# Weighting gathered rows on VectorE, two tiles at once, in place of ScalarE, one tile at a time

## The chip, the cores and the metric

The kernel runs on one core of a Trainium2 chip. The metric is the device time of one execution in microseconds (us). Three executions of the kernel before took 5790.27, 5797.28 and 5843.74 us; the median is 5797.28 us.

## The reference, cut to what matters

Four graph layers follow each other on 3125 nodes of 256 features and 50000 edges that are sorted by their target. The first layer (L0) has three sublayers, and each sends every edge's source row, times the edge's weight, to the edge's target:

```
for l in range(3):
    h = x @ fc_w[l].T + fc_b[l]
    f = einsum('ncd,cde->nce', h.reshape(n, 4, 64) * norm_out, ch_w[l])
    m = f[src] * edge_w[:, None, None]          # 50000 rows of 256, each times one weight
    agg = segment_sum(m, dst, num_segments=n)
    x = relu(agg * norm_in + ch_b[l])
```

The layers behind it (L1, L3) take a maximum over edges with no weight, and L2 is an attention over the same edges. Everything is float32.

## The kernel before, in words

An edge pass walks the 50000 edges (50176 with padding) as 392 tiles of 128 partitions by 256 floats. Each partition holds its own chain of 392 consecutive edges. Four tiles make a group (`GT` = 4), so there are 98 groups (`NG`). The core does seven such passes. Three of them are weighted: e0, e1 and e2, one for each sublayer of L0. Pass e3 (L1) and e5 to e7 (L3) have no weights, and the attention pass (L2) is a function of its own. Node stages lie between the passes.

In a pass, GpSimd issues four indirect DMAs for each group (line 1356). They gather rows of the table in DRAM into the tiles of `G`. A weighted pass has six slots of four tiles (`sets` = 6). A slot comes free when `moved` says so: line 1350 waits until group g-6 has been moved, and the semaphore counts two for each group.

ScalarE moves (`move`, lines 1394 to 1405). It waits for the group's gathers, then for `linked` (the PSUM bank it is about to write, last read two groups before, must have been read), and runs four activations with a scale per partition. Each multiplies one 128x256 tile by its column of `WE` and writes half of a PSUM bank of `mv`; the second one of each pair counts `moved`. `mv` holds two groups.

VectorE links (`link`, lines 1416 to 1438): O[k] = O[k-1] * mask + mv[k], one scalar_tensor_tensor for each tile, each waiting for the one before. It waits for `moved` and, every second group, for the store of the ring slot that it overwrites. SyncE stores pairs of groups (line 1338) from the ring `O` of four groups to DRAM.

Each engine's order is written out. `pipelined` unrolls a list of (function, lead) pairs: at step s it calls each function for group s + lead, in the order of the list. All passes that stand here are flat, so every engine runs straight-line code of 98 steps. On ScalarE the list of a weighted pass is early, `(move, 0)`, late. On VectorE it is early, `(link, 0)`, late. Early and late are work "beside" the pass that has nothing to do with its rows.

In e1 and e2 that work is `rank_beside` (lines 860 to 944), a chain over three engines that does one block k in every two groups. VectorE makes one-hots (two instructions, line 270, late, at the odd step, three steps ahead). TensorE transposes them (`flip`, lines 913 and 914, eight matmuls), ScalarE copies them (`take`, lines 937 to 939, early, at the even step, ahead of its moves), TensorE multiplies them (`meet`, lines 923 to 925), and VectorE evaluates the result (`places`, lines 895 to 902, early, at the odd step, ahead of its links). TensorE's order is `meet` of block k at step 2k, `flip` of block k+1 at step 2k+1. `take` of block k waits for its `flip`; `meet` of block k waits for its `take` and for `places` of block k-1. `mlp_beside` adds four matmuls (line 1699) and one VectorE add (line 1706) in every third group, for 25 groups.

In e0 the work beside is `numbers_and_weights_beside`. Over the first 49 groups it has sixteen one-hot instructions for each group on VectorE (lines 755 and 756), then a number of short chains, and at groups 58 to 89 one scan for each group (line 794).

Of the kernel before, what the change touches and what calls it, by code (L numbers as in the profile page):

```python
# [8 lines left out]
ALU = mybir.AluOpType  # L9
ACT = mybir.ActivationFunctionType  # L10
AX = mybir.AxisListType
ds = bass.ds
# [8 lines left out]
GT = 4  # L21
# [130 lines left out]
def build(nc, a, out):  # L152
    top = ExitStack()
    Stage.used = []
    with top:
# [1128 lines left out]
        def edge_pass(name, index, ops, mask, weighted, beside=nothing_beside, picks=()):  # L1284
# [21 lines left out]
            with Stage(nc, name) as st:  # L1306
# [84 lines left out]

                @block.scalar
                def _(eng):
                    def move(g, q, turn):
                        if g < NG - 1:
                            got[g % sets].arrived(eng, dmas(g))
                        for h in range(2):
                            eng.wait_ge(linked, g * GT + (2 * h + 2))
                            bank = mv[:, 2 * (q % 2) + h, :]
                            for k in range(2):  # L1400
                                if g == NG - 1:
                                    tails[2 * h + k].arrived(eng, 1)
                                last = eng.activation(bank[:, k * D:(k + 1) * D], slot(g, 2 * h + k), ACT.Copy,  # L1403
                                                      scale=WE[:, ds(g * GT + (2 * h + k), 1)])
                            last.then_inc(moved, 1)

                    early, late = beside_on("scalar", eng)
                    steps = [*early, *([(move, 0)] if weighted else []), *late]
                    if steps:
                        pipelined(NG, U, eng, *steps, flat=flat)  # L1410

                @block.vector
                def _(eng):
                    eng.sem_inc(linked, 8)

                    def link(g, q, turn):
                        for k in range(GT):
# [19 lines left out]
                            behind = O[:, q % OB, k - 1, :] if k else O[:, (q - 1) % OB, GT - 1, :]  # L1437
                            eng.scalar_tensor_tensor(O[:, q % OB, k, :], behind, mask[:, ds(g * GT + k, 1)], here, op0, op1).then_inc(linked, 1)  # L1438

                    def lay_out(g, q, turn):  # L1440
                        if g in pick_of:
                            i = pick_of[g]
                            if i >= 2:
                                eng.wait_ge(spread, i - 1)
                            eng.tensor_scalar(diag[:, i % 2, :], ident[:, :], node_of[:, g:g + 1], None, ALU.mult).then_inc(laid, 1)
# [15 lines left out]
                        eng.wait_ge(keyed, 2)  # L1461
                    picking = [(lay_out, 7), (one_hots, 5)] if picks else []
                    early, late = beside_on("vector", eng)
                    pipelined(NG, U, eng, *early, *picking, (link, 0), *late, flat=flat, head=0 if flat else U)
                    if "vector_end" in side:
                        side["vector_end"](eng)
            for q in range(sets):
# [807 lines left out]
```

## Time and profile before

| what | value |
| --- | --- |
| three executions | 5790.27, 5797.28, 5843.74 us |
| the profiled execution's own time | 5809.64 us |
| its span (first to last instruction) | 5807.9 us |
| PE, DVE, ACT, POOL busy | 2840.8, 3248.1, 1029.9, 3239.7 us |
| gathers of e0: first and last start | 110.9 and 717.1 us |
| gathers of e1 | 814.1 and 1444.1 us |
| gathers of e2 | 1542.7 and 2173.2 us |
| gathers of e3 | 2336.4 and 2921.3 us |

In the profile PE is TensorE, DVE is VectorE, ACT is ScalarE, POOL is GpSimd, SP is SyncE. Times are us from the start of the span. "Idle before" is the time that an engine stood still ahead of an instruction, and the arrow names what ended it; "issue" stands where no wait that the profile shows ended it, "remote" where the release came from something that the profile doesn't know. A matmul's start is recorded, its end is modelled.

### The profile page before, as it was taken

How to read it: one execution, taken by the hardware profiler on the slowest of the kernel's cores; microseconds unless marked ns; L12 is line 12 of the kernel's file. 1: busy time of each engine (PE TensorE's matmuls, PEld its weight loads, DVE VectorE, ACT ScalarE, POOL GpSimd, SP SyncE). 2: the span in 40 equal slices, each digit the busy share in tenths (PEclk: the TensorE clock that was granted, in tenths of full speed). 3: DMA queues.
4: the chain of work that ended last, by engine and by line, in shares of the span. 5: the costliest groups of instructions: out<-in, count | busy, mean ns of one | idle time of the engine just before them, and what ended most of it. 6: DMA issues, size and time to landing. Idle time of an engine off the chain costs nothing. (4 is left out here: it accounts for less than half of the span.)

```text
span 5807.9 us, 44153 instructions
## 1 busy us (share of the span) xinstructions
PE 2840.8 (49%) x11716; PEld 2035.6 (35%) x11716; DVE 3248.1 (56%) x9230; ACT 1029.9 (18%) x2648; POOL 3239.7 (56%) x3351
## 2 busy tenths in 40 slices
PE   5111045544455446454451000477676777578675
PEld 4110033333333334221131000356455655466554
DVE  5577434444344445477875777635454555445554
ACT  4223323333233333000011111210001000010002
POOL 5556645555455553666736666246562666536662
PEclk8555565555655557675665555688787988788776
DMA  3445545544455441355524665235452555435552
GB/s 115 156 158 176 183 130 174 168 165 162 132 171 167 169 160 59 126 173 174 184 95 148 192 196 191 75 123 182 167 179 100 170 189 187 157 101 192 186 178 96
DMA packets 284843, 900.76 MB, mean 155 GB/s; under 512 B 70731, under 2 KB 123320, under 8 KB 241464
## 3 DMA queue, kind: packets, MB, share of 16 engines
q0 software_dynamic: 157728, 428.39, 25.5%
q1 hardware_dynamic: 126872, 469.63, 21.0%
q8 instruction: 93, 1.52, 0.1%
q14 instruction: 150, 1.23, 0.1%
HBM read 445.41 MB, written 452.35 MB: 155 GB/s over the span
## 5 line engine op out<-in xcount | busy, mean ns | idle before, releaser
L1356 POOL DMA_INDIRECT WORK<-table,SRCI x1376 | 1315.9, 956 | 1023.2 <-issue 476.2
L1356 POOL DMA_INDIRECT WORK<-table,BYSRC x1092 | 1064.9, 975 | 831.1 <-issue 551.2
L1382 PE MATMUL e_pm<-ARENA 128*128 128x256 f32 (+1 forms) x4200 | 1110.0, 416 | 291.4 <-issue 287.6
L1382 PEld LDWEIGHTS e_pm<-ARENA 128*128 128x128 f32 (+1 forms) x4200 | 860.4, 209 | 518.2 <-issue 402.3
L1438 DVE SCALAR_TENSOR_TENSOR WORK<-WORK,NST,e_mv 128x256 f32<-128x256 f32 x1173 | 562.4, 479 | 411.7 <-issue 199.9
L1438 DVE SCALAR_TENSOR_TENSOR WORK<-WORK,LOWE 128x256 f32<-128x256 f32 x1288 | 626.1, 486 | 103.1 <-remote 38.6
L1403 ACT ACTIVATE e_mv<-WORK,WE 128x256 f32<-128x256 f32 x1176 | 485.9, 458 | 316.7 <-DVE WORK L1438 247.0
L1824 POOL DMA_INDIRECT WORK<-table_attention,SRCI x392 | 375.0, 957 | 181.4 <-issue 127.9
L1438 DVE SCALAR_TENSOR_TENSOR WORK<-WORK,LOWE,e_pm 128x256 f32<-128x256 f32 x84 | 40.3, 480 | 680.3 <-remote 341.5
L923 PE MATMUL e_rb<-ARENA 98*128 98x128 bf16 x392 | 114.8, 293 | 621.0 <-ACT ARENA L939 508.9
L1455 DVE TENSOR_TENSOR ARENA<-e_pr,ARENA 128x640 f32<-128x640 f32 x420 | 314.2, 812 | 69.0 <-remote 41.9
L987 PE MATMUL e_hi<-ARENA 128*128 128x392 bf16 x392 | 180.8, 461 | 332.8 <-DVE ARENA L973 185.1
L923 PEld LDWEIGHTS e_rb<-ARENA 98*128 98x128 bf16 x392 | 95.6, 244 | 648.3 <-ACT ARENA L939 598.5
L895 DVE SCALAR_TENSOR_TENSOR ARENA<-e_rb,upto 128x128 bf16<-128x128 f32 x392 | 90.6, 287 | 380.6 <-remote 338.7
L2013 PE MATMUL comb<-ident,WORK 128*8 128x128 f32 x1 | 0.4, 372 | 595.1 <-PEq L149 595.1
L925 PE MATMUL e_ra<-ARENA 98*128 98x32 f32 x784 | 249.0, 412 | 0.0
L1356 POOL DMA_INDIRECT ARENA<-table,SRCI x192 | 192.1, 1001 | 89.2 <-issue 56.4
L1544 ACT ACTIVATE WORK<-bn_ps 128x256 f32<-128x256 f32 x3 | 1.2, 384 | 1236.3 <-PE bn_ps L1027 1236.3
L925 PEld LDWEIGHTS e_ra<-ARENA 98*128 98x128 f32 x784 | 196.2, 310 | 45.9
L2013 PEld LDWEIGHTS comb<-ident,WORK 128*8 128x8 f32 x1 | 0.1, 84 | 595.2 <-issue 595.2
L1169 PE MATMUL n_x<-WORK 128*128 128x256 f32 x200 | 79.8, 492 | 261.8 <-DVE WORK L1088 195.5
L937 ACT ACTIVATE ARENA<-e_rt 98x512 bf16<-98x512 bf16 x98 | 58.5, 597 | 824.3 <-remote 649.7
(383 smaller groups left out, 5413.0 us busy)
## 6 DMA issues: line engine op xcount, KB each, us to landing
edge_results<-WORK SPq DMA_DIRECT2D x336, 1024.0 KB
edge_results_attention<-WORK SPq DMA_DIRECT2D x98, 544.0 KB
WORK<-table,SRCI POOLq DMA_INDIRECT x1376
table<-ARENA SPq DMA_DIRECT2D x28, 640.0 KB, 3.3
WORK<-table,BYSRC POOLq DMA_INDIRECT x1092
turned_layers<-WORK SPq DMA_DIRECT2D x50, 128.0 KB, 1.7
HTT<-turned_layers SPq DMA_DIRECT2D x50, 128.0 KB
WORK<-table_attention,SRCI POOLq DMA_INDIRECT x392
```

Source lines behind the costliest of these rows:

```text
L895: eng.scalar_tensor_tensor(rank_tmp[:, n, :], pb[:, n * P:(n + 1) * P], 2.0, upto[:, :], ALU.is_equal, ALU.mult, accum_out=rank[:, 0, n:n ...
L923: eng.matmul(pb[:, cols], rank_t[0:HI, b, 0, cols], rank_t[0:HI, b, 0, cols], start=True, stop=False)
L925: last = eng.matmul(pa[:, n * LO:(n + 1) * LO], rank_tf[0:HI, b, cols], HIST[0:HI, ds((k + first) * RB + n, 1), :].rearrange("p o l -> p ( ...
L937: eng.activation(rank_t[0:HI, b, 0, :], turned_hot[0:HI, 0, :], ACT.Copy)
L987: last = eng.matmul(sums[d][:, :], oh_pay[:, q % 2, n, d, :], oh_place[:, q % 2, n, :], start=False, stop=False)
L1169: eng.matmul(xps[:, t % 2, 0:D], SEL[:, slot, :], CARRY if crossing else ENDS, start=True, stop=True).then_inc(crossed, 1)
L1356: eng.indirect_dma_start(slot(g, k), None, T, bass.IndirectOffsetOnAxis(ap=index[:, t:t + 1], axis=0)).then_inc(landed, 16)
L1382: last = eng.matmul(made_ps[:, i % 4, 0:D], hot_rows[0:n, i % 2, j, :], AGG[0:n, j, :], start=j == 0, stop=j == NT - 1)
L1403: last = eng.activation(bank[:, k * D:(k + 1) * D], slot(g, 2 * h + k), ACT.Copy, scale=WE[:, ds(g * GT + (2 * h + k), 1)])
L1438: eng.scalar_tensor_tensor(O[:, q % OB, k, :], behind, mask[:, ds(g * GT + k, 1)], here, op0, op1).then_inc(linked, 1)
L1455: eng.tensor_tensor(hot_rows[:, i % 2, at, :], rows_ps[:, i % 2, 0:P].unsqueeze(1).broadcast_to([P, CH, P]), key[:, at].unsqueeze(2).broad ...
L1824: eng.indirect_dma_start(G[:, q * GT + k, :], None, T2, bass.IndirectOffsetOnAxis(ap=SRCI[:, t:t + 1], axis=0)).then_inc(got[q].sem, 16)
```

## The change

ScalarE's `move` is removed. VectorE gets `scale` with a lead of one group: at step s it scales group s+1 and then links group s. One instruction multiplies two gathered tiles (128x512) by their two columns of `WE`, each column stretched over 256 elements by the access pattern, and writes a whole PSUM bank. `scale` stands behind the early steps and ahead of `link`. It waits for `linked` up to all links of group g-2, and for the gathers; each of its two instructions counts `moved`, so the totals that GpSimd and `link` wait for stay as they were. The buffers, the six slots and the ring stay as well.

```diff
@@ block.scalar
-                    def move(g, q, turn):
-                        if g < NG - 1:
-                            got[g % sets].arrived(eng, dmas(g))
-                        for h in range(2):
-                            eng.wait_ge(linked, g * GT + (2 * h + 2))
-                            bank = mv[:, 2 * (q % 2) + h, :]
-                            for k in range(2):
-                                if g == NG - 1:
-                                    tails[2 * h + k].arrived(eng, 1)
-                                last = eng.activation(bank[:, k * D:(k + 1) * D], slot(g, 2 * h + k), ACT.Copy,
-                                                      scale=WE[:, ds(g * GT + (2 * h + k), 1)])
-                            last.then_inc(moved, 1)
-
                     early, late = beside_on("scalar", eng)
-                    steps = [*early, *([(move, 0)] if weighted else []), *late]
+                    steps = [*early, *late]
@@ block.vector
+                    def scale(g, q, turn):
+
+                        if g >= 2:
+                            eng.wait_ge(linked, g * GT + (8 - GT))
+                        if g < NG - 1:
+                            got[g % sets].arrived(eng, dmas(g))
+                        for h in range(2):
+                            if g == NG - 1:
+                                for k in range(2):
+                                    tails[2 * h + k].arrived(eng, 1)
+                            at = g % sets * GT + 2 * h
+                            eng.tensor_tensor(mv[:, 2 * (q % 2) + h, :].rearrange("p (k d) -> p k d", k=2), G[:, at:at + 2, 0:D],
+                                              WE[:, ds(g * GT + 2 * h, 2)].unsqueeze(2).broadcast_to([P, 2, D]), ALU.mult).then_inc(moved, 1)
+
@@
-                    pipelined(NG, U, eng, *early, *picking, (link, 0), *late, flat=flat, head=0 if flat else U)
+                    pipelined(NG, U, eng, *early, *([(scale, 1)] if weighted else []), *picking, (link, 0), *late, flat=flat, head=0 if flat else U)
```

## Rows read from the trace of the kernel before

**Rows 1.** The page, parts 1 and 5: engines, and the line that goes.
```profile
PE 2840.8 (49%) x11716; PEld 2035.6 (35%) x11716; DVE 3248.1 (56%) x9230; ACT 1029.9 (18%) x2648; POOL 3239.7 (56%) x3351
...
L1403 ACT ACTIVATE e_mv<-WORK,WE 128x256 f32<-128x256 f32 x1176 | 485.9, 458 | 316.7 <-DVE WORK L1438 247.0
```
**Rows 2.** Stretches e0, e1, e2, e3, attention: PE, PEld, DVE, ACT, POOL busy, PEclk, DMA.
```profile
110.00:735.00 625.00, 69.42 (x510) 53.79 (x510) 383.54 (x1412) 173.73 (x405) 374.21 (x392) 0.50 0.51 170
812.00:1466.00 654.00, 321.01 (x1277) 204.26 (x1277) 303.27 (x1056) 230.22 (x539) 371.28 (x392) 0.50 0.49 163
1540.00:2196.00 656.00, 321.96 (x1278) 205.06 (x1279) 303.89 (x1059) 230.21 (x539) 372.20 (x393) 0.50 0.48 163
2330.00:2960.00 630.00, 279.90 (x924) 124.89 (x921) 446.05 (x1541) 10.59 (x29) 391.06 (x392) 0.64 0.49 161
3090.00:3650.00 560.00, 0.00 (x0) 0.00 (x0) 418.84 (x1004) 66.64 (x336) 371.50 (x389) 0.50 0.59 187
```
**Rows 3.** Line 1356 (gathers) in e1: durations, then its engine's idle time by releaser.
```profile
L1356 POOL DMA_INDIRECT WORK<-table,SRCI x392: 941/947/1052, 814.1 to 1444.1; - x196
...
  ACT e_mv L1403: 147.4, 24
```
**Rows 4.** The same of line 1356 in e0.
```profile
L1356 POOL DMA_INDIRECT WORK<-table,SRCI x392: 940/947/2631, 110.9 to 717.1; - x196
...
  ACT e_mv L1403: 112.8, 29
```
**Rows 5.** The same of line 1356 in e3, a pass without weights.
```profile
  DVE WORK L1438: 80.6, 16
```
**Rows 6.** Timeline of POOL in e1: first and last of 16 gathers, and the next.
```profile
1122.05 0.94 POOL L1356 DMA_INDIRECT WORK<-table,SRCI  x1 [6.51 <-ACT e_mv L1403]
...
1140.81 0.94 POOL L1356 DMA_INDIRECT WORK<-table,SRCI  x1 [0.30 <-issue]
1148.18 0.94 POOL L1356 DMA_INDIRECT WORK<-table,SRCI  x1 [6.42 <-ACT e_mv L1403]
```
**Rows 7.** Timeline of ACT over the same cycle.
```profile
1127.33 3.25 ACT L1403 ACTIVATE e_mv<-WORK,WE 128x256 f32<-128x256 f32 x8
1144.81 0.60 ACT L937 ACTIVATE ARENA<-e_rt 98x512 bf16<-98x512 bf16 x1 [14.23 <-remote]
```
**Rows 8.** Timeline of DVE over the same cycle.
```profile
1130.33 0.42 DVE L1706 TENSOR_TENSOR X<-e_mlp,X 128x256 f32<-128x256 f32 x1
1139.09 0.29 DVE L895 SCALAR_TENSOR_TENSOR ARENA<-e_rb,upto 128x128 bf16<-128x128 f32 x1 [8.34 <-remote]
...
1140.67 2.10 DVE L1438 SCALAR_TENSOR_TENSOR WORK<-WORK,NST,e_mv 128x256 f32<-128x256 f32 x4
1142.68 0.76 DVE L270 TENSOR_TENSOR ARENA<-ARENA,iota_b 128x392 bf16<-128x392 bf16 x2
```
**Rows 9.** Timeline of PE over the same cycle: the last matmuls of meet and flip.
```profile
1130.77 0.64 PE L925 MATMUL e_ra<-ARENA 98*128 98x32 f32 x2
...
1132.95 0.29 PE L914 MATMUL e_rt<-identb,ARENA 128*32 128x128 bf16 x1
```
**Rows 10.** Timeline of DVE early in e0: two instructions with no wait.
```profile
142.29 0.28 DVE L755 TENSOR_SCALAR ARENA<-iota_b,BYSRC 128x98 bf16<-128x98 bf16 x1 [1.17 <-issue]
143.69 0.23 DVE L756 TENSOR_SCALAR ARENA<-iota_b,ARENA 128x32 bf16<-128x32 bf16 x1 [1.12 <-issue]
```
**Rows 11.** Timeline late in e0: two groups, by their scans.
```profile
599.25 1.03 DVE L794 TENSOR_TENSOR_SCAN ARENA<-e_hd,start_src,ARENA 98x392 f32<-98x392 f32 x1
...
606.25 1.03 DVE L794 TENSOR_TENSOR_SCAN ARENA<-e_hd,start_src,ARENA 98x392 f32<-98x392 f32 x1
```
**Rows 12.** DVE's groups by form in e0.
```profile
L755 DVE TENSOR_SCALAR ARENA<-iota_b,BYSRC 128x98 bf16<-128x98 bf16 x392 | 101.2, 267 | 23.3 <-issue 23.1
```
**Rows 13.** Timeline of DVE in the attention pass: two products of the same form.
```profile
3308.05 1.26 DVE L1936 TENSOR_TENSOR att_g<-WORK,att_p 128x512 f32<-128x512 f32 x2
```
**Rows 14.** POOL's gathers in the attention pass: busy, mean ns, idle by releaser.
```profile
L1824 POOL DMA_INDIRECT WORK<-table_attention,SRCI x389 | 372.2, 957 | 180.5 <-issue 127.0 <-DVEq L1940 53.5
```

## The prediction

> **What bounds the kernel now.** I read the page first, then the busy times by stretch, then who waits for whom at the gathers, then one cycle on every engine. On the page no engine is busy above 56% and the line that goes, 1176 activations, is 485.9 us of ScalarE, an engine busy 18% of the span [rows 1]. So the change can only pay through a wait. By stretch, each weighted pass takes 625 to 656 us for 392 gathers, e3 takes 630 and the attention pass about 560, and in none of them is VectorE or GpSimd full [rows 2].
>
> Line 1356 says why. In e1 GpSimd waits 24 times for ScalarE, 147.4 us, and is otherwise busy or issuing: 482.6 us without those waits, 1.23 us for a gather [rows 3]. The 24 waits are alike. A cycle is 26.13 us (1122.05 to 1148.18): 16 gathers, four groups, in 19.7 us to the end of the last, and a pause of 6.42 us [rows 6]. In the pause ScalarE isn't working: its last move ends at 1130.6, and it stands 14.23 us until `take` starts at 1144.81 [rows 7]. `take` waits for `flip`, whose last matmul is recorded at 1132.95 [rows 9]. VectorE in the same way starts `places` at 1139.09 after 8.34 us, though `meet` is recorded as done at 1131.4 [rows 8, 9]. Both idles are "remote". So TensorE's results come 8 to 12 us later than the trace models them, and everything in order behind `take` or `places` waits with it.
>
> The same slowness shows in the open on VectorE in e0. Two one-hots with no wait start 1.40 us apart, where one takes 0.27 us [rows 10, 12]; late in e0 a group of ten VectorE instructions takes exactly 7.0 us, 0.70 each, while gathers run on [rows 11]. I read one pattern: while GpSimd issues gathers, an engine gets through some 70 to 80 instructions at full speed, then only one per 0.70 us, and full speed returns about 3 us after GpSimd pauses (last gather over at 1141.75, `take` at 1144.81) [rows 6, 7]. The count is an estimate: attention has about 72 VectorE instructions for each of its pauses (1004 in 14 cycles of 24 to 32 gathers) and e1, with 44 a cycle, never slows on VectorE [rows 2, 14]. In e1 the engine that runs dry is TensorE, with 53 matmuls and 53 loads a cycle.
>
> **The change part by part.**
>
> *Removed:* 392 activations a pass from ScalarE. In e1 and e2 `take` already starts the moment it is released, so rank work gains nothing. What goes is the tie of the slots to `flip` and `take`.
>
> *Added:* two VectorE instructions a group. Attention has two of this form in 1.26 us, PSUM output included [rows 13]; I take 1.26 us a group, 123 us a pass. They free the slots, so they lie on GpSimd's path. Does VectorE become the bound? In e1 two groups cost it `places` 1.58 us (1139.09 to 1140.67), links 4.2, one-hots 0.76, the add 0.28 (0.42 in two of three) [rows 8], and now 2.52: 9.3 us, against 10.0 us for eight gathers at 1.25. It fits, barely. Its instructions rise from 44 to about 52 a cycle: below the 70.
>
> *Moved:* a slot is now freed behind `places` of the block before, so behind `meet`, no longer behind `flip` and `take`. `meet` comes one TensorE step earlier, which sounds like a gain, but the cycle is tied to GpSimd's own pause. Walk it: GpSimd's last gather ends; TensorE is released 3.06 us later [rows 6, 7]; what is left of a slow `meet` finishes; `places` 1.58; the two products 1.26; GpSimd resumes. Before, the same path was 3.06 plus 3.37 for `take` and four moves. How much of `meet` is left is the unknown. Block k+1 comes about 7 us after the release, at full speed (flip 1.8, `take` 1.5, `meet` 3.7, from rows 7 and 9 and the spacing of matmuls there); then TensorE is dry and the next flip and meet are 24 matmuls at 0.70, about 19 us with `take`. That is 26 us from the release, and the next release comes at 3.06 + 2.84 + 19.7 = 25.6 us. So some 0.4 us is left: pause 6.3, cycle 26.1. Bounds: nothing left and a pause as in the passes that VectorE already frees, 80.6/16 = 5.0 us in e3 [rows 5], gives -1.2 us a cycle, -30 a pass; a whole `meet` left, 3.7 us, gives a pause of 9.6, +3.2 a cycle, +76 a pass. I take 0.
>
> *Behind the waits:* `scale` waits for its gathers ahead of the links, the one-hots and, through order, the next `places`. Where GpSimd leads by four groups, as here, they have landed. SyncE's stores wait for links, which come 1.3 us a group later; the ring has two groups of room, so this costs nothing unless VectorE falls under GpSimd's pace. At the end of a pass the backlog of about five groups is worked off by VectorE alone: 5 x 1.26 = +6 us in each pass.
>
> *GpSimd itself:* its gather takes longer beside VectorE instructions that read SBUF twice. In e1 a gather costs 1.23 us without waits; in e3, where all four links and the one-hots do so or run fast modes, (584.9 - 80.6)/391 = 1.29 [rows 3, 5] (584.9: last start of e3 minus the first, from the table). Attention's product reads only one SBUF tensor, so no row has the new form: 0 to 0.056 us a gather, 0 to 22 us a pass. Two instructions in place of sixteen: I take 7 us a pass.
>
> The Trainium skill ("SBUF — State Buffer", on the shared port pair) says that a VectorE instruction with two SBUF inputs and a GpSimd instruction that reads SBUF lock each other out fully. By it each product could hold a gather off for its whole length; that is the rival C below, and e3's 1.29 speaks for a small share of it.
>
> *e0:* early, VectorE has 16 one-hots and four links, about 4.4 us a group at full speed, 5.7 with the products, above GpSimd's 5.0. But time goes in cycles as in e1: about 80 fast instructions, then slow until GpSimd pauses. With 26 instructions a group in place of 23 a cycle holds 3.3 groups, not 4; the slots run out sooner and the pause is shorter (GpSimd's waits there are 112.8/29 = 3.9 us [rows 4]). I make it -10 us over 49 groups. Late, a slow group goes from ten instructions to thirteen, 7.0 to 9.1 us [rows 11]: GpSimd's lead of four groups is used up after nine gathered groups in place of fourteen, a pause restores the speed, and 25 groups come out near 6.4 us in place of 5.5. +24 us. With the 6 and 7 us from above, e0 is +27. Bounds: -50 (the pace of attention) and +123 (all products on the path).
>
> *Sum:* e0 +27, e1 and e2 each 0 + 6 + 7 = +13, in all +53 us on the profiled execution's 5809.6, 5863. That execution is 12.4 us above the median of the runs, so the forecast is about **5850 us**, +0.9%. All else in the kernel (e3, attention, e5 to e7, node stages) is untouched.
>
> **The rivals.** A measurement of this kernel can tell about 1% from no change, 58 us.
>
> *A, faster.* The pauses belong to ScalarE's order (`take` ahead of the moves), and a pass freed by VectorE runs like attention: 53.5 us of waits in 389 gathers against 147.4 [rows 3, 14]. For: attention has the same products on VectorE and a stretch of 560 us. Against: it has no TensorE work at all [rows 2]. Each of e1 and e2 would gain 60 to 90 us, e0 up to 30: about 5640.
>
> *B, slower.* `meet` becomes the tie that decides the pause. If more than about 1 us of it is left at the release, the pause passes 7 us; VectorE at 9.3 of 10 us has no room to catch up. A whole `meet`, +76 a pass, and e0 at +60 give about 6020. For: the 8.34 us wait for it [rows 8] is in VectorE's order now, ahead of the slots. Against: it comes a step ahead of `flip`.
>
> *C, GpSimd locked out.* 588 products, up to 0.63 us each: +370, about 6170. Against: e3's 0.056 us a gather.
>
> *D.* The change doesn't move the bound at all: 5800.
>
> **How the numbers follow.** My forecast with D as its flat variant, between 5780 and 5900, has 0.54; A 0.22; B 0.21; C 0.03. Faster by over 1%: 0.22 from A. Slower by over 1%: B and C 0.24 and a fifth of the forecast, 0.10: 0.34. Within 1%: 0.44. The range leaves half of A's far end and half of B's and all of C out: 5690 to 5990. The forecast's own range is 5780 to 5900.
>
> **What would show it.** ScalarE has 147 activations in e1 and VectorE 196 products of about 0.68 us. Right: GpSimd's waits in e1, now for VectorE, are 22 to 26, of 5.5 to 7 us, in cycles of 16 gathers; VectorE's idle is ahead of line 895; e1's gathers take 625 to 645 us. The walk of the cycle is wrong if the pauses come every 24 gathers (A) or last 9 us (B), or if a gather between pauses costs over 1.29 us (C). e0 shows the late part: scans 9.1 us apart where they are slow. If e0's gathers end sooner than 606 us after they start, the step that counts instructions is wrong.

## The result, and the profile after

The changed kernel takes 5751.59 us, the median of 4 runs (5731.99 to 5771.79), against 5804.25 for the kernel before: a ratio of 0.9895, 95% interval 0.9862 to 0.9928. I had forecast 5850 us, slower by 0.9%. By the ratio it is faster by 1.05%; the two medians lie 0.9% apart. The profiled execution takes 5771.79 us, 37.9 less than the one before.

Page of the kernel after, part 1, and the new group of part 5:

```profile
PE 2826.7 (49%) x11716; PEld 2024.7 (35%) x11716; DVE 3584.6 (62%) x9818; ACT 554.0 (10%) x1472; POOL 3315.3 (57%) x3351
...
L1438 DVE TENSOR_TENSOR e_mv<-WORK,WE 128x512 f32<-128x512 f32 x588 | 383.2, 697 | 52.6 <-DMA WORK<-table,SRCI 45.1
```

ScalarE lost 1176 activations and 476 us, VectorE gained 588 products and 336 us [rows 1]. GpSimd, whose instructions are the same, is busy 75.6 us more. That is a price of the change, and it stands on an engine whose instructions the diff doesn't touch.

GpSimd's group of line 1356 in e1 (busy us, mean ns, idle before by releaser), first of the kernel before, then of the kernel after with the count of its waits for VectorE:

```profile
L1356 POOL DMA_INDIRECT WORK<-table,SRCI x392 | 371.3, 947 | 306.3 <-ACT e_mv L1403 147.4 <-issue 112.3 <-POOLq L149 46.6
```
```profile
L1356 POOL DMA_INDIRECT WORK<-table,SRCI x392 | 394.0, 1005 | 255.8 <-issue 117.1 <-DVE e_mv L1438 91.4 <-POOLq L149 46.2
...
  DVE e_mv L1438: 91.4, 15
```

So e1 is a sum of two: the waits fall from 147.4 to 91.4 us (-56.0), the gathers' own time rises from 371.3 to 394.0 (+22.7), and "issue" by 4.8; one wait of 1.1 us is new and labelled remote. That makes -27.4; the gathers of e1, first start to last, take 602.5 us (793.8 to 1396.3) in place of 630.0. e2 is the same (604.1 for 630.5), and in e0 the waits fall from 112.8 to 59.9 and the gathers grow from 374.2 to 402.1:

```profile
L1356 POOL DMA_INDIRECT WORK<-table,SRCI x392 | 402.1, 1026 | 215.6 <-issue 155.6 <-DVE e_mv L1438 59.9
```

which gives 578.3 us for 606.3. The cycle of e1 is no longer the one of [rows 6]. GpSimd's timeline after, the first gather behind each of three pauses in a row:

```profile
1117.92 0.94 POOL L1356 DMA_INDIRECT WORK<-table,SRCI  x1 [5.71 <-DVE e_mv L1438]
...
1154.97 0.94 POOL L1356 DMA_INDIRECT WORK<-table,SRCI  x1 [5.75 <-DVE e_mv L1438]
...
1191.95 0.94 POOL L1356 DMA_INDIRECT WORK<-table,SRCI  x1 [5.72 <-DVE e_mv L1438]
```

A cycle is 37.0 us and holds 24 gathers; before it was 26.1 us and 16. The pause is 0.7 us shorter, and there are 15 in place of 24. VectorE's and ScalarE's side of one of these pauses, behind a last gather that ends at 1149.2:

```profile
1151.82 0.29 DVE L895 SCALAR_TENSOR_TENSOR ARENA<-e_rb,upto 128x128 bf16<-128x128 f32 x1 [8.57 <-remote]
...
1153.39 1.30 DVE L1438 TENSOR_TENSOR e_mv<-WORK,WE 128x512 f32<-128x512 f32 x2
```
```profile
1151.91 0.60 ACT L937 ACTIVATE ARENA<-e_rt 98x512 bf16<-98x512 bf16 x1 [14.40 <-remote]
```

The end of a pause is as in [rows 7, 8]: everybody stands, and 2.6 us after GpSimd's last gather both engines start within 0.1 us of each other. Now `places` and one group's products are all that is left to do (1151.82 to 1154.7), and GpSimd goes on.

**Where the 37.9 us between the two profiles are.** e0 -28.0, e1 -27.5, e2 -26.4, together -81.9. The stretches behind them grow: from the last gather of e0 to the first of e1 97.0 becomes 104.7, behind e1 98.6 becomes 103.7, behind e2 163.2 becomes 165.5: +15.1. Most of it is the end of the pass: from the end of the last gather to the end of the last link it takes 14.7, 18.1 and 18.2 us before and 23.2, 22.3 and 22.3 after. The rest, +29, is in passes whose code is the same: e3 +3.4, attention +2.8, e5 -9.7, e6 +19.1, e7 +12.0. Those are the pauses' own scatter: in a second pair of profiles (runs 5 and 6) e5 to e7 went the other way, 1662.7 us before and 1650.4 after. So the change is worth 67 us in the first pair of profiles (81.9 less 15.1) and 68 in the second (89.6 less 21.1, counted the same way), and the rest is scatter.

### The profile page after: what moved, and what is told of

Read it like the earlier page. It is cut to its first block and busy times, and to the rows that moved or that the text cites. A ratio compares the mean times of both kernels' runs of the same rounds, so it can differ in the third digit from the quotient of the medians.

```text
span 5770.0 us, 43557 instructions
## 1 busy us (share of the span) xinstructions
PE 2826.7 (49%) x11716; PEld 2024.7 (35%) x11716; DVE 3584.6 (62%) x9818; ACT 554.0 (10%) x1472; POOL 3315.3 (57%) x3351
## 5 line engine op out<-in xcount | busy, mean ns | idle before, releaser
L1356 POOL DMA_INDIRECT WORK<-table,SRCI x1376 | 1390.7, 1011 | 864.0 <-issue 481.4
L1438 DVE TENSOR_TENSOR e_mv<-WORK,WE 128x512 f32<-128x512 f32 x588 | 383.2, 697 | 52.6 <-DMA WORK<-table,SRCI 45.1
L925 PEld LDWEIGHTS e_ra<-ARENA 98*128 98x128 f32 x784 | 196.2, 310 | 45.8
L1954 DVE SCALAR_TENSOR_TENSOR WORK<-WORK,NST,att_g 128x256 f32<-128x256 f32 x343 | 164.9, 481 | 57.4 <-remote 12.6
L987 PEld LDWEIGHTS e_hi<-ARENA 128*128 128x128 bf16 x392 | 48.3, 123 | 432.8 <-DVE ARENA L973 240.0
```

The lines of the kernel that those rows point to most:

```text
L925: last = eng.matmul(pa[:, n * LO:(n + 1) * LO], rank_tf[0:HI, b, cols], HIST[0:HI, ds((k + first) * RB + n, 1), :].rearrange("p o l -> p ( ...
L987: last = eng.matmul(sums[d][:, :], oh_pay[:, q % 2, n, d, :], oh_place[:, q % 2, n, :], start=False, stop=False)
L1356: eng.indirect_dma_start(slot(g, k), None, T, bass.IndirectOffsetOnAxis(ap=index[:, t:t + 1], axis=0)).then_inc(landed, 16)
L1438: eng.tensor_tensor(mv[:, 2 * (q % 2) + h, :].rearrange("p (k d) -> p k d", k=2), G[:, at:at + 2, 0:D], WE[:, ds(g * GT + 2 * h, 2)].unsqu ...
L1954: eng.scalar_tensor_tensor(OA[:, i, t, 0:D], OA[:, i, t - 1, 0:D] if t else scaled_row, NST[:, ds(b * BT + t, 1)], here, ALU.mult, ALU.add ...
```

## The experiments

One thing has to be said first. The runs fell on seven chips, and they are of two kinds. On four of them the kernel before takes 5789 to 5826 us, with the pauses described above. On three it takes 4708 or 4709 us and **has no pause at all**. The lines below say which it was. What differs in these chips or in how they are set up, no trace shows. The packets of the gathers' queue take alike on both: 25.5% of sixteen engines' 5807.9 us in the kernel before and 31.2% of their 4717.9 us in run 7, 1481 and 1472 us. Runs 1 and 7 differ from the kernel before only in ScalarE's order, so run 7 stands in for its profile on such a chip. It is 1090 us shorter: 796 of them in the eight passes of gathers, the other 294 between and around the passes, where GpSimd issues such DMAs as well (line 1068).

| run | chip | kernel us | before us | ratio, 95% interval | e1 gathers us | mean gather ns |
|---|---|---|---|---|---|---|
| 1, 7 moves ahead | no pauses | 4712.67; 4718.13 | 4707.74; 4709.11 | 1.0012 [1.0002, 1.0022]; 1.0020 [1.0009, 1.0031] | 491.2; 490.4 | 952; 950 |
| 11 moves ahead | pauses | 5840.52 | 5800.41 | 1.0086 [1.0056, 1.0116] | 641.7 | 962 |
| 2, 8 idle moves | no pauses | 4812.02; 4810.12 | same as 1; 7 | 1.0217 [1.0200, 1.0234]; 1.0214 [1.0197, 1.0231] | 515.5; 514.8 | 1013; 1012 |
| 12 idle moves | pauses | 5697.01 | 5800.41 | 0.9836 [0.9793, 0.9878] | 593.9 | 1006 |
| 3, 10 scale by tile | no pauses | 4763.99; 4769.82 | same as 1; 7 | 1.0115 [1.0098, 1.0131]; 1.0124 [1.0107, 1.0141] | 491.7; 490.9 | 953; 951 |
| 4, 9, 17 eight slots | no pauses | 4805.18; 4810.93; 4802.12 | 4707.74; 4709.11; 4708.93 | 1.0206; 1.0209; 1.0203 [1.0186, 1.0220] | 512.6; 513.1; 511.6 | 1006; 1007; 1004 |
| 5 after again | pauses | 5745.67 | 5816.95 | 0.9895 [0.9850, 0.9939] | 596.7 | 1006 |
| 6 before again | pauses | 5837.93 (one) | 5816.95 | - | 631.5 | 947 |
| 13 flip twice | pauses | 5736.12 | 5788.82 | 0.9909 [0.9887, 0.9932] | 597.3 | 1009 |
| 14 split | pauses | 5779.02 | 5788.82 | 0.9977 [0.9960, 0.9994] | 602.5 | 949 |
| 15 paced | pauses | 5830.94 | 5826.24 | 1.0008 [0.9981, 1.0035] | 625.9 | 946 |
| 16 rests | pauses | 5729.04 | 5826.24 | 0.9854 [0.9793, 0.9916] | 598.7 | 958 |
| 18 rests, more | no pauses | 5164.37 | 4708.93 | 1.0974 [1.0955, 1.0992] | 597.5 | 955 |

**Runs 1, 7 and 11: ScalarE's moves ahead of `take`.** Kernel before, one line:

```diff
-                    steps = [*early, *([(move, 0)] if weighted else []), *late]
+                    steps = [*([(move, 1)] if weighted else []), *early, *late]
```

> The kernel before, with one change of order: ScalarE still scales the rows with its 392 activations a pass, but one group ahead, and its moves stand ahead of take in its queue, so that a slot is freed behind places of the block before, as in the changed kernel. Theory ORDER (what the change brought is that the slots no longer hang behind flip and take): GpSimd's pauses in e1 come every 24 gathers instead of 16, 15 to 17 of them of 5.5 to 6 us in place of 24 of 6.1, and the gather stays at 1.235 us, so e1's gathers take 575 to 595 us in place of 630; the kernel 5620 to 5700 us, faster than both. Theory COUNT (an engine, or all of them together, gets through a fixed number of instructions between pauses, and the change took 392 activations off that number): nothing changes, pauses every 16 gathers, e1 625 to 635 us, the kernel 5780 to 5830.

> The kernel of run 1 once more (the moves on ScalarE one group ahead, ahead of take), on a chip where the kernel before has its pauses and takes about 5800 us, if the call gets one. Theory ORDER: pauses every 24 gathers in e1 and e2, 15 to 17 of them, gathers at 1.235 to 1.256 us, e1 575 to 595 us, ratio 0.97 to 0.985. Theory COUNT (ScalarE's activations shorten the cycle): pauses every 16, e1 620 to 635 us, ratio 0.99 to 1.005. Without pauses on this chip: as in run 1, ratio 1.001.

> The kernel of runs 1 and 7 (the moves stay on ScalarE, one group ahead and ahead of take); both of those fell where the kernel before has no pauses. With pauses: theory ORDER expects them every 24 gathers in e1 and e2, 15 to 17 of them, gathers at 1.235 to 1.256 us, e1 575 to 595 us, ratio 0.97 to 0.985; theory COUNT expects every 16 gathers, e1 620 to 635 us, ratio 0.99 to 1.005. Without pauses: ratio 1.001 to 1.002.

Runs 1 and 7 fell on chips without pauses and say only that the order costs 0.1 to 0.2% there. GpSimd's group in e1 of run 7:

```profile
L1356 POOL DMA_INDIRECT WORK<-table,SRCI x392 | 372.3, 950 | 140.7 <-issue 114.8 <-POOLq L149 21.6 <-ACT e_mv L1403 4.3
```

No wait for ScalarE is left in 392 gathers but 4.3 us, and the pass takes 490 us, where the pass of [rows 3], on a chip with pauses, took 630. Run 11 is the test. Its group in e1:

```profile
L1356 POOL DMA_INDIRECT WORK<-table,SRCI x392 | 377.2, 962 | 312.2 <-ACT e_mv L1403 152.1 <-issue 113.4 <-POOLq L149 46.8
...
  ACT e_mv L1403: 152.1, 22
```

22 waits of 6.9 us, still one in 16 gathers. Theory ORDER falls: the tie to `take` and `flip` was not what held the cycle at 16, and with it falls the explanation that I would have given for the gain.

**Runs 2, 8 and 12: activations put back on ScalarE on which nothing depends.** Kernel after, e1 and e2:

```diff
-                    steps = [*early, *late]
+                    spare, = carve(AGW_BASE[:, 4600:6648], ((2, GT, D), F32))
+
+                    def idle_moves(g, q, turn):
+                        for h in range(2):
+                            if g >= 2:
+                                eng.wait_ge(idled, 2 * (g - 2) + h + 1)
+                            for k in range(2):
+                                last = eng.activation(spare[:, q % 2, 2 * h + k, :], MB[:, :], ACT.Copy)
+                            last.then_inc(idled, 1)
+                    steps = [*early, *([(idle_moves, 0)] if name in ("e1", "e2") else []), *late]
```

> The changed kernel, with as many activations put back on ScalarE in e1 and e2 as before the change, at the same place behind take and with as many waits and signals, but on constant rows into spare memory, so that no slot depends on them. Theory ORDER: no effect, e1's gathers 600 to 605 us with pauses every 24 gathers, the kernel 5730 to 5770. Theory COUNT with ScalarE's instructions in the common number: pauses every 16 to 20 gathers again, e1 over 615 us, the kernel 5780 to 5850. Theory COUNT by engine (only TensorE's own number matters): as ORDER.

> The kernel of run 2 once more (the changed kernel with 392 activations put back in e1 and e2 on which nothing depends). With pauses: ORDER expects every 24 gathers, e1 595 to 605 us, as the changed kernel; COUNT expects cycles of 16 to 20 gathers and over 615 us. Without pauses: ratio 1.022 as in run 2.

> The kernel of runs 2 and 8 (the changed kernel, with 392 activations put back in e1 and e2 on which nothing depends). With pauses: ORDER expects them every 24 gathers, e1 595 to 605 us, ratio 0.985 to 0.995, as the changed kernel; COUNT expects cycles of 16 to 20 gathers and over 615 us, ratio 0.995 to 1.01. Without pauses: ratio 1.021.

Run 12, e1:

```profile
L1356 POOL DMA_INDIRECT WORK<-table,SRCI x392 | 394.4, 1006 | 247.3 <-issue 114.6 <-DVE e_mv L1447 85.9 <-POOLq L149 46.7
```

16 waits, 85.9 us: with ScalarE as loaded as before the change, the cycle stays at 24 gathers. Freeing ScalarE is not what the change gave. In e2 of this run the 16 waits are shorter, 72.7 us in all, and the pass takes 581.6 us where the changed kernel's takes 604; why is open. Runs 2 and 8 show the changed kernel's code, whole, with these activations added, on chips without pauses: slower than before by 2.1%.

**Runs 3 and 10: one large SBUF input per product.** Kernel after:

```diff
-                            at = g % sets * GT + 2 * h
-                            eng.tensor_tensor(mv[:, 2 * (q % 2) + h, :].rearrange("p (k d) -> p k d", k=2), G[:, at:at + 2, 0:D],
-                                              WE[:, ds(g * GT + 2 * h, 2)].unsqueeze(2).broadcast_to([P, 2, D]), ALU.mult).then_inc(moved, 1)
+                            for k in range(2):
+                                last = eng.tensor_scalar(mv[:, 2 * (q % 2) + h, k * D:(k + 1) * D], slot(g, 2 * h + k),
+                                                         WE[:, ds(g * GT + 2 * h + k, 1)], None, ALU.mult)
+                            last.then_inc(moved, 1)
```

> The changed kernel, but each product is made for one tile, by a tensor_scalar with the weight as a column per partition: four instructions of 128x256 a group with one large SBUF input in place of two of 128x512 with two SBUF inputs. Theory CONTENTION (a gather is stretched while VectorE reads two SBUF inputs): the mean gather in e1 falls from 1.005 to 0.95-0.96 us and the cost without pauses from 1.300 to 1.235-1.25; with pauses unchanged that is 18 to 25 us less in each weighted pass, the kernel 5670 to 5710. Rival (any VectorE work on slots or into PSUM stretches them, or the links do): the gather stays at 0.99 to 1.01 us, the kernel 5740 to 5790. Two more instructions a group could shorten the cycle if VectorE's count decides: pauses every 20 gathers.

> The kernel of run 3 once more (four products a group, each with one large SBUF input). Run 3 had gathers of 0.953 us in e1 against 1.006 to 1.013 in runs 2 and 4. With pauses: the gather back at 0.95 and 1.24 to 1.26 without pauses, so e1 is 15 to 25 us shorter than the changed kernel's 597 to 603 if the pauses stay every 24 gathers, ratio 0.975 to 0.985 with e0 no worse; if eight more VectorE instructions a cycle shorten it to 20 gathers, 595 to 615 us. Without pauses: ratio 1.011 as in run 3.

GpSimd in e1, of run 10 and then of run 17, which has the two-input products of the change; both without pauses, so that a pass is nothing but its gathers (the last two slots of run 17 lie in another tensor, so its gathers stand in two groups):

```profile
L1356 POOL DMA_INDIRECT WORK<-table,SRCI x392 | 372.7, 951 | 140.7 <-issue 117.6 <-POOLq L149 21.6 <-DVE e_mv L1438 1.5
```
```profile
L1356 POOL DMA_INDIRECT WORK<-table,SRCI x296 | 297.5, 1005 | 112.0 <-issue 89.9 <-POOLq L149 22.1
L1356 POOL DMA_INDIRECT ARENA<-table,SRCI x96 | 95.9, 999 | 29.2 <-issue 29.2
```

951 ns against 1004, and 1013 and 1012 in runs 2 and 8, whose slots are six. Contention is shown: the same multiplication, at the same place on the same engine, with one large input costs GpSimd nothing in e1 (490.9 us, as run 7), and with two it costs 21 us. The products of run 10 are also shorter (128x256), so length would be a rival; the attention pass rules it out, below. In e0 the four smaller instructions cost as much as contention did (549.5 us in run 10, 548.4 in run 17): there VectorE is full, and run 10 waits 15 times, 45.8 us.

The trace shows how it happens. After, GpSimd and VectorE in e1:

```profile
1124.56 0.94 POOL L1356 DMA_INDIRECT WORK<-table,SRCI  x1 [0.30 <-issue]
1125.81 1.33 POOL L1356 DMA_INDIRECT WORK<-table,SRCI  x1 [0.30 <-issue]
1127.44 0.94 POOL L1356 DMA_INDIRECT WORK<-table,SRCI  x1 [0.30 <-issue]
```
```profile
1125.03 1.30 DVE L1438 TENSOR_TENSOR e_mv<-WORK,WE 128x512 f32<-128x512 f32 x2
```

The products end at 1126.33, and the gather that started inside them at 1125.81 ends at 1127.14, 0.81 us later. The gather before it was under way when the products began, and took its 0.94. Over e1, 78 of the 392 gathers start inside a product and last 1.245 us on average; the other 314 last 0.946, as before the change. Each of the 78 ends 0.81 to 0.87 us after the product in which it began. The products last 0.69 us on average whether a gather is under way at their start or not. So a gather is held only if it begins during a product, until about the product's end, and then still needs 0.81 us.

The attention pass of the kernel before has products of the same form and length, but with one input in PSUM. A gather of it that begins inside such a pair, and the pair:

```profile
3304.02 0.95 POOL L1824 DMA_INDIRECT WORK<-table_attention,SRCI  x1 [0.30 <-issue]
...
3303.89 1.28 DVE L1936 TENSOR_TENSOR att_g<-WORK,att_p 128x512 f32<-128x512 f32 x2
```

79 gathers of that pass begin inside a product, and they last 0.946 us. So it is the second SBUF input that holds a gather, not the product's length.

The Trainium skill ("SBUF — State Buffer", section "SBUF: two separate sides") says that a VectorE instruction with two SBUF inputs and a GpSimd one that reads SBUF exclude each other: whichever starts first has the shared pair of ports for its whole instruction. For the gathers that begin inside a product, the trace agrees. That a gather under way holds the product back, it does not show (0.69 us either way), and there the measurement decides.

**Runs 4, 9 and 17: eight groups of slots in e1 and e2** (two more, behind the rank work's part of the arena; kernel after):

```diff
-            sets = SETS if weighted or picks else DEEP
+            sets = 8 if name in ("e1", "e2") else SETS if weighted or picks else DEEP
```

> The changed kernel with 8 groups of slots in place of 6 in e1 and e2. Theory SLOTS (GpSimd runs through its slots while everything behind TensorE stands, so the cycle is as long as the slots allow): pauses every 32 gathers, about 12 of 5.7 us in place of 16, e1 575 to 585 us, the kernel 5700 to 5725. Theory COUNT (a number of instructions between pauses): pauses stay every 24 gathers, or TensorE's results come late for longer and the pause stays, e1 598 to 606 us, the kernel 5735 to 5770.

> The kernel of run 4 once more (8 groups of slots in e1 and e2). With pauses: theory SLOTS expects cycles of 32 gathers, 11 to 13 pauses of 5 to 6 us, e1 575 to 590 us; COUNT expects cycles of 24 gathers or a pause no shorter in the sum, 595 to 605 us. Without pauses: ratio 1.020 as in run 4.

> The kernel of runs 4 and 9 (the changed kernel with 8 groups of slots in e1 and e2), for a chip with pauses. Theory SLOTS (after VectorE stops getting results on time, GpSimd runs on until its slots are used up, so two more groups make the cycle 32 gathers): 11 to 13 pauses of 5 to 6.2 us, e1 391 x 1.30 + 70 = 575 to 590 us, ratio 0.975 to 0.985. Rival ONSET (what decides is when the others' lateness begins, and it ends only with a pause): cycles stay at 24 gathers or become uneven, e1 597 to 610 us, ratio 0.985 to 0.995.

All three fell on chips without pauses, so the question that they were for stays open. What they give is what the change costs where nothing pauses: e0 takes 548.4 us in run 17 and 492.3 in run 18, whose e0 is the code before; e1 511.6 against 490.4 to 491.2. That is +56, +21 and +21, 98 us in all, and the kernel is 2.0% slower (93 us). The changed kernel by itself was not run on such a chip.

**Runs 5 and 6: both kernels again.**

> The changed kernel itself, timed again. In the four runs above no pass of GpSimd's gathers had the pauses of 5 to 6 us that the first profiles show, and the kernel before took 4708 us, so the same chip type can run this kernel with and without them. Theory PAUSES (the gain came from fewer pauses, its price is longer gathers): where the pauses are absent, only the price is left: gathers of 1.005 us in e1 and e2 and about 1.07 in e0, 20 to 23 us longer in e1 and in e2, 55 us longer in e0, the kernel 1.018 to 1.024 of before; where the pauses are there, 0.985 to 0.995 of before, as first measured. Rival (the gain doesn't come from pauses at all): under 1.000 in both conditions.

> The kernel before itself, for its profile beside the changed kernel's on one chip. Without pauses: e0, e1 and e2 at 1.256 us a gather, 491 to 493 us a pass, no wait for ScalarE of over 1.5 us, 4700 to 4715 us. With pauses: as first profiled, 606, 630 and 630 us, 5790 to 5850 us.

With pauses, 0.9895 once more, with e0, e1 and e2 at 579.2, 596.7 and 604.4 us after and 608.3, 631.5 and 630.1 before. That is what theory PAUSES expects where there are pauses. Its other side, 1.018 to 1.024 without them, is seen only in kernels that add something to the changed one (runs 2, 4, 8, 9 and 17: 1.020 to 1.022).

**Run 13: each flip's transposes twice.** Kernel after:

```diff
-                        for n in range(RB):
+                        for n in (*range(RB), *range(RB)):
                             eng.transpose(turned_hot[0:HI, 0, n * P:(n + 1) * P], rank_hi[:, b, n, :], identb[:, :])
```

> The changed kernel, with the eight transposes of each flip issued twice in e1 and e2 (392 more matmuls with their loads in a pass; the second set writes the same values). TensorE isn't full: 1277 matmuls in a pass of about 600 us. Theory TENSORE (after a pause TensorE works at full speed for a limited number of matmuls, then at 0.70 us each until the next pause): 1277 matmuls fit as 725 at the slow pace in 508 us of gathers and 16 x 34.5 after pauses; 1669 then need about 27 pauses, every 14 to 16 gathers, and e1 takes 650 to 680 us, ratio 1.00 to 1.02. Theory LINKS (VectorE's or the slots' own state sets the cycle, TensorE's count does not matter): pauses stay every 24 gathers, e1 597 to 610 us, ratio 0.985 to 0.995. On a chip without pauses: no effect, ratio 1.02 to 1.023.

```profile
L1356 POOL DMA_INDIRECT WORK<-table,SRCI x392 | 395.6, 1009 | 249.3 <-issue 114.5 <-DVE e_mv L1438 88.3 <-POOLq L149 46.5
```

392 more matmuls with their loads in the pass don't shorten the cycle: 16 waits, 88.3 us, 24 gathers a cycle. That takes away the core of my reading of the trace, that in e1 TensorE "runs dry" after some 53 matmuls.

**Run 14: the change in e1 and e2 alone, by tile** (the products of runs 3 and 10; in e0 ScalarE scales).

> The change in e1 and e2 alone, and there with four products a group of one tile each (one large SBUF input); in e0 ScalarE scales as before. Without pauses: e0 492 us, e1 and e2 491 us, so the price of the change is gone, ratio 0.999 to 1.002. With pauses: e0 as before (606 us), gathers in e1 and e2 at 0.95 us and 1.25 us without pauses. If the cycle stays at 24 gathers, e1 and e2 580 to 590 us and ratio 0.983 to 0.988; if four more VectorE instructions a block of two groups shorten it to 20 gathers, 595 to 610 us and 0.99 to 0.995.

```profile
L1356 POOL DMA_INDIRECT WORK<-table,SRCI x392 | 372.1, 949 | 277.8 <-issue 112.4 <-DVE e_mv L1450 109.5 <-POOLq L149 46.4
```

The gathers are back at 949 ns, and with them the cycle is back at 16 gathers (22 pauses of 5.4 us): what contention no longer costs is paid in pauses, and e1 takes 602.5 us, as with the change. Behind its gathers more is left to do: from the last gather of e1 to the first of e2 it takes 115.5 us (98.6 before, 103.7 after), behind e2 175.5 (163.2 and 165.5). So the kernel is only 0.2% faster than before, where 0.5 to 1.7% were expected. Two things differ from the change here, the second input and the number of products in a group, four in place of two. This run doesn't separate them.

**Run 15: a memset behind each gather.** Kernel before, e1 and e2: `eng.memset(AGW_BASE[:, 4600 + t:4601 + t], 0.0)`.

> The kernel before, with one small memset (128x1) on GpSimd behind each gather of e1 and e2, so that a gather costs 1.30 to 1.37 us instead of 1.235; ScalarE still moves the rows. Theory PACE (a slower gather lets the other engines run on time longer, and that made 16 gathers into 24): pauses every 24 gathers, 15 or 16 of them of 6 us, e1 391 x 1.30 to 1.37 + 95 = 600 to 630 us, ratio 0.99 to 1.00. Rival FORM (the number or the engine of the scaling instructions decides, the pace doesn't): pauses stay every 16 gathers, e1 391 x 1.30 to 1.37 + 147 = 655 to 685 us, ratio 1.01 to 1.02. On a chip without pauses: 508 to 536 us, ratio 1.007 to 1.02.

The experiment failed in its aim. The memset (0.12 us) fell into the 0.30 us of issue, and a gather still cost 1.235 us. The cycles became shorter (29 pauses of 4.9 us in place of 24 of 6.1), the sum of the pauses stayed, 143 us, and so did the pass, 626 us.

**Run 16: GpSimd breaks off by itself.** Kernel before, e1 and e2:

```diff
+                        if name in ("e1", "e2") and g % 3 == 2:
+                            for h in range(2):
+                                if g > 2 or h:
+                                    eng.wait_ge(rested, 2 * (g // 3) + h)
+                                eng.memset(AGW_BASE[:, 4600:6500], 0.0).then_inc(rested, 1)
```

> The kernel before, with GpSimd breaking off by itself after every 12 gathers in e1 and e2, for two memsets of 128x1900 in a row (3.4 us by the 1.37 us of 128x1536 at the kernel's start), before the slots are used up. Theory RELEASE (the other engines come back to speed 3 us after GpSimd stops its gathers, whatever it does meanwhile): hardly a wait for ScalarE is left, e1 391 x 1.235 + 32 x 3.5 = 595 us in place of 630, ratio 0.985 to 0.99. Rival (GpSimd must be idle, or the others' lateness comes from something else): the rests add up, e1 630 + 50 to 110 us, ratio 1.02 to 1.04. On a chip without pauses: 491 + 110 us, ratio 1.045.

GpSimd's timeline and its group in e1:

```profile
1123.34 0.95 POOL L1356 DMA_INDIRECT WORK<-table,SRCI  x1 [0.30 <-issue]
1124.29 3.43 POOL L1362 MEMSET ARENA<- 128x1900 f32 x2
1127.88 0.95 POOL L1356 DMA_INDIRECT WORK<-table,SRCI  x1 [0.15 <-issue]
...
L1356 POOL DMA_INDIRECT WORK<-table,SRCI x392 | 375.4, 958 | 160.4 <-issue 113.1 <-POOLq L149 46.1 <-ACT e_mv L1408 1.2
```

147.4 us of waits have become 1.2, for 108 us of memsets; e1 takes 598.7 us where 595 was expected. It looks as if on such a chip the gathers need stops of some 3 us, and GpSimd pays less if it stops early than if it is stopped: a forced pause is 6.1 us because behind the release stand `take` and four moves. GpSimd need not be idle in the stop; memsets do. The lateness isn't gone altogether: VectorE still has 16 remote waits of over 1 us in e1, but they add up to 36.8 us and none is longer than 2.6, where before they were 27 with 184.1 us. Part of the gain lies behind the gathers: from the last of e1 to the first of e2 it takes 88.0 us in place of 98.6. This kernel, the one before with rests added to GpSimd's program, is as fast as the changed one (0.9854 and 0.9895, intervals that overlap).

**Run 18: rests in e3 and e5 to e7 as well**, six memsets of 128x512 behind every 20 gathers.

> The kernel of run 16 (GpSimd breaks off for 3.4 us after every 12 gathers in e1 and e2; ScalarE scales as before), and in e3 and e5 to e7 it breaks off as well, for six memsets of 128x512 (about 3.2 us) after every 20 gathers. Theory RELEASE: no wait of over 1.5 us for VectorE is left there, e3 391 x 1.29 + 19 x 3.4 = 569 us in place of 585, e5 to e7 363 x 1.27 + 18 x 3.4 = 522 in place of 543 to 566; ratio 0.965 to 0.98. Rival (20 gathers are already past the point where the others are late, so the rest ends in the same backlog): waits of 1 to 3 us stay behind the rests, e5 to e7 540 to 560 us, ratio 0.98 to 0.99.

It met a chip without pauses, where a rest is pure cost: 1.097. But its e1 takes 597.5 us there, and run 16's takes 598.7 on a chip with pauses. With the rests in, e1 takes the same on both kinds of chip. Whether they help in e3 and e5 to e7 where there are pauses, this run can't say.

## Why the prediction was wrong, step by step

- **"The cycle is tied to GpSimd's own pause" and stays at 26.1 us: wrong, and most of the error.** The walk through the end of the pause was right: a release about 3 us behind the last gather (2.6), `places` 1.57, two products 1.3, in all 5.7 us with 0.3 of issue, where I had 6.3. But its other half, when the next lateness begins, rested on a count of instructions, and I held that count fixed. It isn't fixed: the cycle grew to 24 gathers, 37.0 us, and the pauses fell from 24 to 15. Had it stayed at 16, e1 would by this estimate have had 24 pauses of 5.7 us and come out at 630 + 23 - 11, about 642.
- **The count itself.** "70 to 80 instructions, then one per 0.70 us" describes VectorE in e0 [rows 10 to 12], but as a rule it is refuted for TensorE (run 13) and for ScalarE (run 12). Its support was also misread. Attention before has 16 pauses of over 1.5 us, in cycles of 16 to 28 gathers, not 14 of 24 to 32, so 63 VectorE instructions for each and not 72. And the units differ: of the "ten VectorE instructions" between two scans in [rows 11] the trace counts five (four links and a scan), while the 44 and 72 are such counted instructions. Nor is VectorE's own number fixed: the trace has 43 of them in the cycle of [rows 6] and 77 in one after. The sign set for this step, e0's gathers over in under 606 us, came true: 578.3.
- **Contention, "I take 7 us a pass" within 0 to 22: mis-sized.** It is 22.7 us in e1 with pauses, three times the term and just above its upper bound, 21 without, and 28 (56 without pauses, with what VectorE's fullness adds) in e0. I divided by instructions ("two in place of sixteen"); what counts is the share of time in which a gather can begin inside a product: 196 products, 0.60 us apart within a pair, cover about 118 of 602 us, a fifth, and 78 of 392 gathers is a fifth.
- **The backlog, +6 a pass: right in size.** From the last gather to the last link it takes 8.5, 4.2 and 4.1 us more in e0, e1 and e2. Its reason, five groups times 1.26 us, isn't shown: that time is 34.2 us in e1 of run 14 and 4.6 in run 16, so it depends on how late the other engines are when the pass ends, and without pauses e1 has 8.5 us (run 17) against 12.3 (run 7).
- **e0, +27 us: wrong in sign (-28.0).** Its first 49 groups gained 20.8 us, where I had put 10; the late part then gained 7.2, where I had put a loss of 24. The price of a slow group was nearly right, 9.1 forecast and 9.8 measured between the scans, but only three groups pay it, where before 17 or so stand 7.0 apart [rows 11]. Timeline of VectorE late in e0, first where I expected slow groups, then where they are:

```profile
590.41 1.03 DVE L794 TENSOR_TENSOR_SCAN ARENA<-e_hd,start_src,ARENA 98x392 f32<-98x392 f32 x1
594.55 1.03 DVE L794 TENSOR_TENSOR_SCAN ARENA<-e_hd,start_src,ARENA 98x392 f32<-98x392 f32 x1
...
662.32 1.03 DVE L794 TENSOR_TENSOR_SCAN ARENA<-e_hd,start_src,ARENA 98x392 f32<-98x392 f32 x1
672.12 1.03 DVE L794 TENSOR_TENSOR_SCAN ARENA<-e_hd,start_src,ARENA 98x392 f32<-98x392 f32 x1
```

  The nine pauses behind the first scan, 24.0 us, have become one of 2.4. It is the same step that failed: lateness begins later than a fixed count says.
- **Rival A** named the sign that I had set, pauses every 24 gathers. But its reason, ScalarE's order, fell in run 11, and its size, 60 to 90 us in each of e1 and e2, left out contention: the waits fell by 56 us in e1, the pass by 27.
- **Rival C** is right as a mechanism and wrong in its size: a product holds a gather, but only one that begins inside it. The sign set for it, a gather of over 1.29 us between pauses, came true as well: 1.30.

**What stays open** is why the lateness begins later in the changed kernel. Shown: it is neither the tie to `take` (run 11), nor ScalarE's load (12), nor TensorE's count (13), and it does go with the two-input form, or with two products a group in place of four (14). What goes along in all of these is the gathers' own cost: cycles of 16 gathers where a gather costs 1.235 to 1.252 us without waits (before, runs 11 and 14), of 24 where it costs 1.30 (after, runs 5, 12 and 13) and about 23 in e3 before, at 1.29. It would fit that gathers which follow each other more slowly let the others run on time for longer, and then the contention pays for itself. But run 15, meant to slow the gathers alone, did not slow them, so this is argued, not shown, and other passes speak against it as the whole reason: attention before has mostly cycles of 24 gathers at 1.26 us, e5 to e7 mostly of 26 at 1.27. What makes the other engines late at all is open too. That they wait for the loading of their own instructions was not tested: the instruction queues carry the same 28 packets during e1's gathers in the kernel before and in run 7, at 0.1% of the DMA engines' time in both, but whether an engine waited for one, no view shows. Whether the number of slots plays a part was not tried where there are pauses.

## What to carry to other kernels

When an engine stands idle in regular pauses, find what ends them and what begins them, and don't take a count read off one case for the second: the pause's end could be walked in three steps from the trace, its beginning could not, and that decided the sign. Before moving a multiplication to VectorE beside a stream of GpSimd gathers, look at its inputs: with one large SBUF input it cost the gathers nothing in e1, with two it held every fifth one. In e0, where VectorE is full, the smaller instructions cost as much. And measure on more than one chip: this change is 1% faster where the pauses are, and its code, with small additions, 2% slower where they are not.

## What the runs showed of the hardware that was not expected

- Chips of one type run this kernel in 4708 or in 5789 to 5826 us. Some 800 us of the difference are pauses in the passes of gathers (e1 takes 490 us on one kind and 630 on the other), some 290 lie in the stages between them.
- A stop of 3.4 us in the gathers, every 12 of them, takes away nearly all the time that GpSimd waits (147.4 us became 1.2 in e1, run 16), though GpSimd is busy with memsets in it. Of VectorE's remote waits in e1 36.8 us are left of 184.1.
- A gather is held by a two-input VectorE product only if it begins inside it (78 gathers at 1.245 us, the other 314 at 0.946), and the product takes 0.69 us whether a gather is under way or not. A product of the same length with one input in PSUM doesn't hold it (79 gathers at 0.946, attention before).
- A 128x1 memset of 0.12 us between two gathers costs no time: a gather still comes every 1.235 us between pauses (run 15), as the 0.30 us of issue between them cover it.
